# The expert stage of a graph and mixture-of-experts kernel: one TensorE signal a step, seven steps deep instead of five

## The chip, the cores and the metric

The kernel runs on one core of a Trainium2 chip. The metric is the time of one execution on the device in microseconds (us). Before the change it is 2094.08, the median of three runs (2093.04 to 2095.15).

## What is computed

The input is x (128 graphs of 128 nodes, 384 values a node, fp32) and an adjacency matrix a graph. A two-layer graph network comes first and is not touched. Then follows the expert layer, which the change is about:

```python
xt = layernorm(x).reshape(-1, 384)                  # 16384 tokens
route_prob = softmax((xt @ enc_w + enc_b) @ sw_w + sw_b)
routes = argmax(route_prob)                         # one of 8 experts
h = gelu(xt @ w1[expert] + b1[expert])              # 384 -> 64
out = (h @ w2[expert] + b2[expert]) * max(route_prob)   # 64 -> 384
x = x + out
```

## The kernel before

Two blocks follow each other. The first computes the graph network over the 128 graphs, decides each token's expert, and scatters each token's row (its 384 values, then the layer norm's scale and shift, the probability and the token's number: 388 words) into DRAM buckets, one for each expert. The second block, the expert stage (from line 1357), works through 72 tiles of 256 tokens, each of one expert. A tile has T = 2 halves of 128 tokens, and a feature row has C = 3 chunks of 128.

Each engine has its own instruction stream, which a Python loop writes out in full: `tiles` calls `step(i)` for i from 0 to 76, and in step i an engine works on the tile that the pipeline's depth gives it. The order within an engine is the order of the calls; between engines there are only semaphores. For tile j:

- SyncE (`load`, L1421) loads the tile's rows into `tok[j % 8]`. From tile 8 on it waits until the results (`y_ready`) and ids of tile j - 8 are done.
- ScalarE and VectorE (`normalise`, L1492 and L1541, step j) scale and shift one half each into `n2_rows`.
- TensorE (`turn`, step j + 1) transposes the six 128 x 128 pieces, the first two chunks into one PSUM bank and the third into another (L1445), and signals `turned`.
- ScalarE copies expert and bias weights (`pick_w1`, L1500 and L1504) and the first two chunks (`copy_first`, L1510), VectorE the third (`copy_last`, L1548), into `n2T`, still in step j + 1.
- TensorE (`hidden`, step j + 2, L1457) multiplies by w1: three products of 256 columns, then signals `hidden_done`.
- ScalarE takes the gelu (`gelu`, L1519, step j + 2). VectorE splits it into a high and a low part (`gelu_high`, L1554, and `gelu_low`, L1558, step j + 2).
- GpSimd adds up the row numbers for the store (`keep_ids`, L1597, step j + 2).
- TensorE (`output`, step j + 4, L1469 and L1470) makes two products of 384 columns for each half, and signals `y_done` for each half. Each half has one PSUM bank and waits until VectorE has read that half of the tile before (`y_ready`).
- VectorE (`combine`, L1567, step j + 5) scales the result, adds the token's row, writes `out_rows[j % 4]` and signals `y_ready` for each half.
- GpSimd (`store`, L1607, step j + 5) writes each half to its tokens' places with an indirect DMA, for which it makes the descriptors itself.

Within a step TensorE does turn, hidden, output. ScalarE does normalise, pick, copy, gelu; VectorE does combine, normalise, copy, split. So ScalarE copies what TensorE turned in the same step, and takes the gelu of what TensorE multiplied in the same step. SyncE waits at the end for all stores (L1431), and a barrier ends the program (L1412).

## Time and profile before

| | |
|---|---|
| median of three runs | 2094.08 us |
| the profiled execution's own time | 2095.15 us |
| its span, first to last instruction | 2093.4 us |
| mean granted TensorE clock | 0.989 |
| busy: TensorE, VectorE, ScalarE, GpSimd | 97%, 81%, 70%, 67% |
| expert stage: first transposes, last results, last store | 1885.70, 2082.25, 2089.22 us |
| token loads, indirect stores | 72 of 388 KB, 144 |

The profile is one execution, with times counted from its first instruction. The durations below come from it alone; its own time is 1.07 us above the median of the runs. In its rows PE is TensorE, DVE VectorE, ACT ScalarE, POOL GpSimd and SP SyncE, and buffer numbers are left out of names: `bank` is any PSUM bank, `n_rows` is n2_rows, `w_top` is w2_top, `w_pick` is w1_pick. A matmul of full fp32 is recorded as two, so that `x6` at L1457 is three products. The end of a matmul is modelled, so the distance between starts is what tells its cost.

### The profile page before, as it was taken

How to read it: one execution, taken by the hardware profiler on the slowest of the kernel's cores; microseconds unless marked ns; L12 is line 12 of the kernel's file. 1: busy time of each engine (PE TensorE's matmuls, PEld its weight loads, DVE VectorE, ACT ScalarE, POOL GpSimd, SP SyncE). 2: the span in 40 equal slices, each digit the busy share in tenths (PEclk: the TensorE clock that was granted, in tenths of full speed). 3: DMA queues.
4: the chain of work that ended last, by engine and by line, in shares of the span. 5: the costliest groups of instructions: out<-in, count | busy, mean ns of one | idle time of the engine just before them, and what ended most of it. 6: DMA issues, size and time to landing. Idle time of an engine off the chain costs nothing. (4 is left out here: it accounts for less than half of the span.)

```text
span 2093.4 us, 48362 instructions
## 1 busy us (share of the span) xinstructions
PE 2029.2 (97%) x12059; PEld 1880.2 (90%) x12059; DVE 1689.7 (81%) x5206; ACT 1468.5 (70%) x3804; POOL 1403.7 (67%) x3342
## 2 busy tenths in 40 slices
PE   5999999999999999999999999999999999959997
PEld 4988899999999999999999999999999999948996
DVE  4788888888888888888888888888888888758997
ACT  4777777777677777777777776777777777627775
POOL 2556666666766666666666676666676666646887
PEclk9999999999999999999999999999999999979999
DMA  7011111221111111111111111111111111118895
GB/s 200 24 37 43 48 43 44 87 81 43 52 52 44 51 52 52 43 48 48 46 45 52 48 43 52 51 43 52 52 49 42 52 48 39 39 64 260 281 297 187
DMA packets 94358, 153.43 MB, mean 73 GB/s; under 512 B 17621, under 2 KB 70875, under 8 KB 94082
## 3 DMA queue, kind: packets, MB, share of 16 engines
q1 hardware_dynamic: 75972, 99.61, 16.4%
q0 software_dynamic: 17408, 50.62, 6.3%
q8 instruction: 103, 1.69, 0.3%
q14 instruction: 171, 1.40, 0.2%
q10 hardware_dynamic: 704, 0.10, 0.0%
HBM read 96.11 MB, written 57.32 MB: 73 GB/s over the span
## 5 line engine op out<-in xcount | busy, mean ns | idle before, releaser
L422 PE MATMUL bank<-wT_hi,own_hi 128*128 128x384 f32 x1536 | 513.6, 334 | 2.4 <-ACT bank L646 2.4
L424 PE MATMUL bank<-wT_hi,own_lo 128*128 128x384 f32 x1536 | 514.1, 335 | 0.0
L423 PE MATMUL bank<-wT_lo,own_hi 128*128 128x384 f32 x1536 | 513.2, 334 | 0.0
L436 PE MATMUL bank<-own_hi 128*128 128x512 f32 x768 | 324.0, 422 | 6.3 <-ACT bank L660 6.1
L438 PE MATMUL bank<-own_hi,own_lo 128*128 128x512 f32 x768 | 302.7, 394 | 0.0
L437 PE MATMUL bank<-own_lo,own_hi 128*128 128x512 f32 x768 | 300.2, 391 | 0.0
L422 PEld LDWEIGHTS bank<-wT_hi,own_hi 128*128 128x128 f32 x1536 | 288.4, 188 | 3.1 <-issue 1.9
L423 PEld LDWEIGHTS bank<-wT_lo,own_hi 128*128 128x128 f32 x1536 | 288.4, 188 | 0.0
L424 PEld LDWEIGHTS bank<-wT_hi,own_lo 128*128 128x128 f32 x1536 | 288.3, 188 | 0.0
L667 ACT ACTIVATE bank<-bank,sum_own 128x384 f32<-128x384 f32 x256 | 141.2, 552 | 206.7 <-issue 177.1
L1190 POOL TENSOR_TENSOR own_lo<-hT,own_hi 128x384 fp32r<-128x384 f32 x256 | 260.6, 1018 | 19.0 <-ACT own_hi L710 18.6
L1272 POOL TENSOR_TENSOR var_e<-mv,denom_sq 128x1 f32<-128x1 f32 x256 | 48.6, 190 | 235.7 <-DVE mv L858 235.6
L639 ACT ACTIVATE bank<-bank,neg_max 128x128 f32<-128x128 f32 x256 | 87.6, 342 | 164.6 <-DVE neg_max L826 164.6
L841 DVE CUSTOM_DVE_ANT_0 diagonal<-delta,ident 128x128 f32<-128x128 f32 x256 | 177.6, 694 | 9.0
L438 PEld LDWEIGHTS bank<-own_hi,own_lo 128*128 128x128 f32 x768 | 144.4, 188 | 33.3
L436 PEld LDWEIGHTS bank<-own_hi 128*128 128x128 f32 x768 | 145.1, 189 | 30.2 <-issue 7.2
L1607 POOL DMA_INDIRECT out_dram<-out_rows,row_ids x144 | 142.5, 989 | 43.9 <-issue 26.4
L1247 POOL TENSOR_SCALAR_AFFINE_SELECT deltaT_hi<-turned_hi 128x128 fp32r<-128x128 f32 x256 | 75.1, 293 | 141.7 <-ACT turned_hi L691 138.8
L660 ACT COPY bank<-own_seed 128x512 f32<-128x512 f32 x256 | 151.3, 591 | 22.5 <-ACT bank L667 0.4
L437 PEld LDWEIGHTS bank<-own_lo,own_hi 128*128 128x128 f32 x768 | 145.8, 190 | 22.9
L1236 POOL DMA_INDIRECT buckets<-rows,dest_words x128 | 138.8, 1084 | 29.4 <-issue 25.0
L863 DVE SCALAR_TENSOR_TENSOR bank<-bank,mv,gamma 128x384 f32<-128x384 f32 x256 | 157.9, 617 | 0.0
(213 smaller groups left out, 5590.1 us busy)
## 6 DMA issues: line engine op xcount, KB each, us to landing
tok<-buckets SPq DMA_DIRECT2D x72, 388.0 KB
x_in<-in_x_dram SPq DMA_DIRECT2D x128, 192.0 KB, 2.6
x_res<-in_x_dram SPq DMA_DIRECT2D x128, 192.0 KB
adj_in<-in_adj_dram SPq DMA_DIRECT2D x128, 64.0 KB, 2.6
buckets<-pads SPq DMA_DIRECT2D x9, 388.0 KB
out_dram<-out_rows,row_ids POOLq DMA_INDIRECT x144
buckets<-rows,dest_words POOLq DMA_INDIRECT x128, 2.8
w_top<-in_L_ffn_w_dram SPq DMA_DIRECT2D x2, 768.0 KB
```

Source lines behind the costliest of these rows:

```text
L422: pe.matmul(o, hi, w_hi(l, m, c), start=False, stop=False, skip_group_check=True)
L423: pe.matmul(o, hi, w_lo(l, m, c), start=False, stop=False, skip_group_check=True)
L424: last = pe.matmul(o, lo, w_hi(l, m, c), start=False, stop=(c == C - 1), skip_group_check=True)
L436: pe.matmul(own_bank[:], hi, own_w_hi, start=False, stop=False, skip_group_check=True)
L437: pe.matmul(own_bank[:], hi, own_w_lo, start=False, stop=False, skip_group_check=True)
L438: last = pe.matmul(own_bank[:], lo, own_w_hi, start=False, stop=(c == C - 1), skip_group_check=True)
L660: act.copy(own_bank[:], own_seed[:, u[1], WINDOW[k]]).then_inc(selfseed_ready, 1)
L667: act.activation(ctx_banks[odd][:, 0:D], own_bank[:, SELF[odd]], ACT.Copy, scale=sum_own[odd][:, 0:1]).then_inc(selfterm_ready, 1)
L841: dve.tensor_tensor_reduce(diagonal[:], delta[:], ident[:], 1.0, 0.0, ALU.mult, ALU.add, sum_own[odd][:]).then_inc(own_ready, 1)
L863: dve.scalar_tensor_tensor(o, o, mv[odd][:, 0:1], gamma[:, w[1], :], ALU.subtract, ALU.mult).then_inc(centred, 1)
L1190: pool.tensor_tensor(own_lo[:, l, :, SLOT[odd]], hT[:].rearrange("p (c t) -> p c t", c=C), own_hi[:, l, :, SLOT[odd]].bitcast(F32), ALU.su ...
L1607: pool.indirect_dma_start(out.rearrange("b s d -> (b s) d"), bass.IndirectOffsetOnAxis(ap=row_ids[k][:, t:t + 1].bitcast(U32), axis=0), ou ...
```

## The change

The pipeline grows from five steps to seven, and TensorE increments one semaphore, `products_done`, on the last matmul of its step, in place of `turned`, `hidden_done` and twice `y_done`. Whoever needs a product of TensorE waits until the step that made it has ended and so works in the next step: turning in step j + 1 as before, copies in j + 2, hidden products in j + 3, gelu in j + 4, split and row ids in j + 5, output products in j + 6, results and stores in j + 7. TensorE does hidden, turn, output within a step. ScalarE begins a step with the copy, then gelu, normalise, pick; VectorE does copy, combine, normalise, split.

The eight PSUM banks are dealt anew: two for the first two chunks, one (was two) for the third, two for hidden products, three (was two) for the results, taken in turn over the halves. `n2_rows`, `w1_pick` and `b1_pick` have three buffers instead of two, `tok` and `row_ids` twelve instead of eight, so SyncE may load twelve tiles before it waits. The core of the diff (the like edits of `normalise`, `pick_w1`, `gelu`, the splits, `keep_ids` and `store` are left out; the last two are called in steps j + SPLIT and j + DEPTH):

```diff
-    OUT_RING = 4
-    tok = ring_sb(RING, "tok", [P, T, WORDS])
-    n2_rows = ring_sb(2, "n2_rows", [P, T, D])
+    OUT_RING, HELD = 4, 12
+    assert TILES % HELD == 0
+    tok = ring_sb(HELD, "tok", [P, T, WORDS])
+    n2_rows = ring_sb(3, "n2_rows", [P, T, D])
...
-    w1_pick = ring_sb(2, "w1_pick", [P, C, 2, R])
-    b1_pick = ring_sb(2, "b1_pick", [P, 1])
+    w1_pick = ring_sb(3, "w1_pick", [P, C, 2, R])
+    b1_pick = ring_sb(3, "b1_pick", [P, 1])
...
-    y_done, y_ready = sem("y_done"), sem("y_ready")
-
-    turn_banks = ((bank[0], bank[1]), (bank[2], bank[3]))
-    hidden_banks = (bank[4], bank[5])
-    y_banks = (bank[6], bank[7])
-
-    OUTPUT, GELUS, DEPTH = 4, 4, 5
...
+    products_done, y_ready = sem("products_done"), sem("y_ready")
+
+    first_banks, last_bank = (bank[0], bank[1]), bank[2]
+    hidden_banks = (bank[3][:, 0:TILE], bank[4][:, 0:TILE])
+    y_banks = (bank[5], bank[6], bank[7])
+
+    PICK, TURN, COPY, HIDDEN, GELU, SPLIT, OUTPUT, DEPTH = 1, 1, 2, 3, 4, 5, 6, 7
+    GELUS = 4
...
+            def load(j):
+                k = j % HELD
                 row = sp.value_load(tile_row[0:1, j:j + 1], min_val=0, max_val=TAIL)
-                if past(j, RING):
-                    sp.wait_ge(y_ready, T * (j - RING) + T)
+                if j >= HELD:
+                    sp.wait_ge(y_ready, T * (j - HELD) + T)
                     sp.nop(nofuse=True)
-                    sp.wait_ge(ids_kept, j - RING + 1)
...
-            def turn(j, k):
+            def turn(j):
                 pe.wait_ge(n2_act_ready, j + 1)
                 pe.wait_ge(n2_dve_ready, j + 1)
-                if past(j, 2):
+                if j >= 2:
                     pe.wait_ge(first_copied, j - 1)
-                    pe.wait_ge(last_copied, j - 1)
-                first, last_bank = turn_banks[k % 2]
                 for c in range(C):
-                    o = first[:, c * TILE:(c + 1) * TILE] if c < 2 else last_bank[:, 0:TILE]
+                    if c == 2 and j >= 1:
+                        pe.wait_ge(last_copied, j)
+                    o = first_banks[j % 2][:, c * TILE:(c + 1) * TILE] if c < 2 else last_bank[:, 0:TILE]
                     for t in range(T):
                         last = pe.transpose(o[:, t * P:(t + 1) * P],
-                                            n2_rows[k % 2][:, t, c * P:(c + 1) * P], ident[:])
-                last.then_inc(turned, 1)
-
-            def hidden(j, k):
+                                            n2_rows[j % 3][:, t, c * P:(c + 1) * P], ident[:])
+                return last
+
+            def hidden(j):
                 pe.wait_ge(w1_picked, j + 1)
                 pe.wait_ge(first_copied, j + 1)
                 pe.wait_ge(last_copied, j + 1)
-                if past(j, 2):
+                if j >= 2:
                     pe.wait_ge(gelu_ready, j - 1)
-                o = hidden_banks[k % 2][:, 0:TILE]
                 for c in range(C):
-                    last = pe.matmul(o, w1_pick[k % 2][:, c, :, :].rearrange("p h r -> p (h r)"),
-                                     n2T[k % 2][:, c, :], start=(c == 0), stop=(c == C - 1))
-                last.then_inc(hidden_done, 1)
-
-            def output(j, k):
+                    last = pe.matmul(hidden_banks[j % 2], w1_pick[j % 3][:, c, :, :].rearrange("p h r -> p (h r)"),
+                                     n2T[j % 2][:, c, :], start=(c == 0), stop=(c == C - 1))
+                return last
+
+            def output(j):
                 e = expert_in(words, j)
                 pe.wait_ge(gelu_top_ready, j + 1)
                 pe.wait_ge(gelu_bottom_ready, j + 1)
                 for t in range(T):
-                    if past(j, 1):
-                        pe.wait_ge(y_ready, T * (j - 1) + t + 1)
-                    o, rows = y_banks[t][:, 0:D], slice(t * P, (t + 1) * P)
-                    pe.matmul(o, gelu_top[k % GELUS][:, rows], w2_top[:, e, :], start=True, stop=False)
-                    pe.matmul(o, gelu_bottom[k % GELUS][:, rows], w2_bottom[:, e, :], start=False, stop=True
-                              ).then_inc(y_done, 1)
-
-            def step(i, k):
-                if there(i - 1):
-                    turn(i - 1, k - 1)
-                if there(i - 2):
-                    hidden(i - 2, k - 2)
+                    n = T * j + t
+                    if n >= 3:
+                        pe.wait_ge(y_ready, n - 2)
+                    o, rows = y_banks[n % 3][:, 0:D], slice(t * P, (t + 1) * P)
+                    pe.matmul(o, gelu_top[j % GELUS][:, rows], w2_top[:, e, :], start=True, stop=False)
+                    last = pe.matmul(o, gelu_bottom[j % GELUS][:, rows], w2_bottom[:, e, :], start=False, stop=True)
+                return last
+
+            def step(i):
+                if there(i - HIDDEN):
+                    last = hidden(i - HIDDEN)
+                if there(i - TURN):
+                    last = turn(i - TURN)
                 if there(i - OUTPUT):
-                    output(i - OUTPUT, (k - OUTPUT) % RING)
+                    last = output(i - OUTPUT)
+                if TURN <= i < TILES + OUTPUT:
+                    last.then_inc(products_done, 1)

             pe.wait_ge(tiles_ready, 2)
             words = read_words(pe)
@@ -1485,48 +1486,50 @@
...
+            def copy_first(j):
+                act.wait_ge(products_done, j + TURN)
+                if j >= 2:
...
-            def step(i, k):
+                act.activation(gelu_out[j % 2][:], hidden_banks[j % 2], ACT.Gelu,
+                               bias=b1_pick[j % 3][:, 0:1]).then_inc(gelu_ready, 1)
+
+            def step(i):
+                if there(i - COPY):
+                    copy_first(i - COPY)
+                if there(i - GELU):
+                    gelu(i - GELU)
                 if there(i):
-                    normalise(i, k)
-                if there(i - 1):
-                    pick_w1(i - 1, k - 1)
-                    copy_first(i - 1, k - 1)
-                if there(i - 2):
-                    gelu(i - 2, k - 2)
+                    normalise(i)
+                if there(i - PICK):
+                    pick_w1(i - PICK)

             act.wait_ge(tiles_ready, 2)
             words = read_words(act)
@@ -1534,50 +1537,52 @@
...
+            def copy_last(j):
+                dve.wait_ge(products_done, j + TURN)
+                if j >= 2:
+                    dve.wait_ge(products_done, j - 2 + HIDDEN)
...
-            def combine(j, k):
+            def combine(j):
+                k, n = j % HELD, j % OUT_RING
+                dve.wait_ge(products_done, j + OUTPUT)
                 for t in range(T):
...
-            def step(i, k):
+            def step(i):
+                if there(i - COPY):
+                    copy_last(i - COPY)
                 if there(i - DEPTH):
-                    combine(i - DEPTH, (k - DEPTH) % RING)
+                    combine(i - DEPTH)
                 if there(i):
-                    normalise(i, k)
-                if there(i - 1):
-                    copy_last(i - 1, k - 1)
-                if there(i - 2):
-                    gelu_high(i - 2, k - 2)
-                    gelu_low(i - 2, k - 2)
+                    normalise(i)
+                if there(i - SPLIT):
+                    gelu_high(i - SPLIT)
+                    gelu_low(i - SPLIT)

             for k in range(GELUS):
                 dve.memset(gelu_bottom[k][HIGH:P, :].bitcast(F32), 0.0).then_inc(ones_set, 1)
@@ -1589,17 +1594,17 @@
```

On TensorE one step of the steady part stood so before (L1445 turns, L1457 is hidden, L1469 and L1470 are the output, whose `REGISTER_ALU` and `ISA` rows work out the expert's place in w2):

```order
L1445 MATMUL bank<-ident,n_rows 128x128 [waits first_copied,last_copied,n2_dve_ready,n2_act_ready]
L1445 MATMUL bank<-ident,n_rows 128x128 x5
L1457 MATMUL bank<-n2T,w_pick 128x256 [waits last_copied,gelu_ready,first_copied,w1_picked]
L1457 MATMUL bank<-n2T,w_pick 128x256 x2
L1469 REGISTER_ALU [waits y_ready,gelu_bottom_ready,gelu_top_ready]
L1469 REGISTER_ALU
L1469 ISA
L1469 MATMUL bank<-w_top,gelu_top 128x384
L1470 REGISTER_ALU
L1470 MATMUL bank<-w_bottom,gelu_bottom 128x384
L1469 MATMUL bank<-w_top,gelu_top 128x384 [waits y_ready]
L1470 MATMUL bank<-w_bottom,gelu_bottom 128x384
```

and stands so now (L1455 hidden, L1444 turns, L1468 and L1469 output):

```order
L1455 MATMUL bank<-n2T,w_pick 128x256 [waits last_copied,gelu_ready,first_copied,w1_picked]
L1455 MATMUL bank<-n2T,w_pick 128x256 x2
L1444 MATMUL bank<-ident,n_rows 128x128 [waits first_copied,n2_dve_ready,n2_act_ready]
L1444 MATMUL bank<-ident,n_rows 128x128 x3
L1444 MATMUL bank<-ident,n_rows 128x128 [waits last_copied]
L1444 MATMUL bank<-ident,n_rows 128x128
L1468 REGISTER_ALU [waits y_ready,gelu_bottom_ready,gelu_top_ready]
L1468 REGISTER_ALU
L1468 ISA
L1468 MATMUL bank<-w_top,gelu_top 128x384
```

The hidden products moved ahead of the transposes, and the wait for VectorE's copy of the third chunk moved from the first transpose to the fifth.

On ScalarE, at the start of the stage, before (L1510 copies the first two chunks, L1492 normalises, L1500 and L1504 pick weights, L1519 is the gelu):

```order
L1510 COPY n2T0<-bank0 128x512 [waits turned]
L1492 ACTIVATE n2_rows2<-tok2 128x384 [waits turned,tok_loaded2]
L1500 REGISTER_ALU x2
L1500 ISA
L1500 COPY w1_pick1<-w1_all 128x384
L1504 ISA
L1504 COPY b1_pick1<-b1_col 128x1
L1510 COPY n2T1<-bank2 128x512 [waits turned]
L1519 ACT_TABLE_LOAD [waits b1_picked]
L1519 ACTIVATE gelu_out0<-bank4,b1_pick0 128x256 [waits hidden_done]
```

and now, from the second copy on:

```order
L1512 COPY n2T1<-bank1 128x512 [waits products_done]
L1494 ACTIVATE n2_rows0<-tok3 128x384 [waits products_done,tok_loaded3]
L1502 REGISTER_ALU x2
L1502 ISA
L1502 COPY w1_pick2<-w1_all 128x384
L1506 ISA
L1506 COPY b1_pick2<-b1_col 128x1
L1512 COPY n2T0<-bank0 128x512 [waits products_done]
L1521 ACT_TABLE_LOAD [waits b1_picked]
L1521 ACTIVATE gelu_out0<-bank3,b1_pick0 128x256 [waits products_done]
```

The load of the gelu's table and the first gelu moved from behind the second copy to behind the third, and that copy waits for TensorE's third step.

## Rows read from the trace of the kernel before

**Rows 1.** The page, busy time of each engine, with its share of the span

```profile
PE 2029.2 (97%) x12059; PEld 1880.2 (90%) x12059; DVE 1689.7 (81%) x5206; ACT 1468.5 (70%) x3804; POOL 1403.7 (67%) x3342
```

**Rows 2.** Busy time by stretch: stretch, engines, granted clock, DMA share, GB/s

```profile
1905.00:2055.00 150.00, 150.00 (x904) 138.76 (x903) 140.39 (x340) 115.46 (x282) 122.01 (x169) 1.00 0.92 291
```

**Rows 3.** Timeline of TensorE, one step: start, us, engine, line, operation

```profile
1951.16 0.82 PE L1445 MATMUL bank<-ident,n_rows 128*128 128x128 f32 x6
1951.81 1.46 PE L1457 MATMUL bank<-n2T,w_pick 128*128 128x256 f32 x6
...
1953.28 0.34 PE L1470 MATMUL bank<-w_bottom,gelu_bottom 128*128 x1
1953.46 0.34 PE L1469 MATMUL bank<-w_top,gelu_top 128*128 x1
1953.63 0.34 PE L1470 MATMUL bank<-w_bottom,gelu_bottom 128*128 x1
1953.81 0.82 PE L1445 MATMUL bank<-ident,n_rows 128*128 128x128 f32 x6
```

**Rows 4.** Timeline of GpSimd in the steady part: three stores, and one after a stall

```profile
1953.97 1.01 POOL L1607 DMA_INDIRECT out_dram<-out_rows,row_ids  x1 [0.16 <-POOL row_ids L1597]
1955.28 0.97 POOL L1607 DMA_INDIRECT out_dram<-out_rows,row_ids  x1 [0.30 <-issue]
...
1956.63 1.00 POOL L1607 DMA_INDIRECT out_dram<-out_rows,row_ids  x1 [0.16 <-POOL row_ids L1597]
...
2049.54 0.97 POOL L1607 DMA_INDIRECT out_dram<-out_rows,row_ids  x1 [1.51 <-DVE out_rows L1567]
```

**Rows 5.** Timeline of GpSimd at the start: the first store of tiles 0, 1 and 2

```profile
1897.28 1.01 POOL L1607 DMA_INDIRECT out_dram<-out_rows,row_ids  x1 [9.02 <-DVE out_rows L1567]
...
1900.23 0.99 POOL L1607 DMA_INDIRECT out_dram<-out_rows,row_ids  x1 [0.20 <-issue]
...
1902.93 0.99 POOL L1607 DMA_INDIRECT out_dram<-out_rows,row_ids  x1 [0.16 <-issue]
```

**Rows 6.** Timeline of the end: GpSimd's stores, VectorE's last results

```profile
2077.60 0.99 POOL L1607 DMA_INDIRECT out_dram<-out_rows,row_ids  x1 [0.16 <-issue]
...
2080.26 0.99 POOL L1607 DMA_INDIRECT out_dram<-out_rows,row_ids  x1 [0.16 <-issue]
...
2082.25 1.14 DVE L1567 SCALAR_TENSOR_TENSOR out_rows<-bank,tok 128x384 f32<-128x384 f32 x2 [0.66 <-PE bank L1470]
...
2087.94 0.97 POOL L1607 DMA_INDIRECT out_dram<-out_rows,row_ids  x1 [0.30 <-issue]
2089.22 0.97 POOL L1607 DMA_INDIRECT out_dram<-out_rows,row_ids  x1 [0.31 <-issue]
```

**Rows 7.** Timeline of TensorE at the start: the second tile's hidden products

```profile
1891.10 1.46 PE L1457 MATMUL bank<-n2T,w_pick 128*128 128x256 f32 x6
```

**Rows 8.** Timeline of ScalarE at the start: the second copy, table load, first gelu

```profile
1888.83 0.58 ACT L1510 COPY n2T<-bank 128x512 f32<-128x512 f32 x1
1889.43 1.28 ACT L1519 ACT_TABLE_LOAD   x1
1890.72 0.47 ACT L1519 ACTIVATE gelu_out<-bank,b_pick 128x256 f32<-128x256 f32 x1
```

**Rows 9.** Timeline of VectorE: results of tiles 0, 1, 2, a result and copy, tile 67

```profile
1895.83 1.12 DVE L1567 SCALAR_TENSOR_TENSOR out_rows<-bank,tok 128x384 f32<-128x384 f32 x2
...
1898.79 1.13 DVE L1567 SCALAR_TENSOR_TENSOR out_rows<-bank,tok 128x384 f32<-128x384 f32 x2
...
1901.21 1.12 DVE L1567 SCALAR_TENSOR_TENSOR out_rows<-bank,tok 128x384 f32<-128x384 f32 x2
...
1949.69 0.60 DVE L1567 SCALAR_TENSOR_TENSOR out_rows<-bank,tok 128x384 f32<-128x384 f32 x1
...
1950.60 0.41 DVE L1548 COPY n2T<-bank 128x256 f32<-128x256 f32 x1
...
2074.09 1.13 DVE L1567 SCALAR_TENSOR_TENSOR out_rows<-bank,tok 128x384 f32<-128x384 f32 x2
```

More of the change, by code:

```diff
@@ L1372, in build @@
             out_rows = ring_sb(OUT_RING, "out_rows", [P, T, D])
-            row_ids = ring_sb(RING, "row_ids", [P, T], I32)
-            tok_loaded = [sem(f"tok_loaded{k}") for k in range(RING)]
+            row_ids = ring_sb(HELD, "row_ids", [P, T], I32)
+            tok_loaded = [sem(f"tok_loaded{k}") for k in range(HELD)]
             stored = [sem(f"stored{k}") for k in range(OUT_RING)]
@@ L1405, in there @@
             def there(j):
-                return not isinstance(j, int) or 0 <= j < TILES
-            def past(j, n):
-                return not isinstance(j, int) or j >= n
+                return 0 <= j < TILES
             with nc.Block() as block:
@@ L1487, in _, with normalise @@
                 def _(act):
-                    def normalise(j, k):
-                        act.wait_ge(tok_loaded[k], 16 // RING * (j - k) + 16)
-                        if past(j, 2):
-                            act.wait_ge(turned, j - 1)
-                        act.activation(n2_rows[k % 2][:, 0, :], tok[k][:, 0, 0:D], ACT.Identity,
+                    def normalise(j):
+                        k = j % HELD
+                        act.wait_ge(tok_loaded[k], 16 * (j // HELD) + 16)
+                        if j >= 3:
+                            act.wait_ge(products_done, j - 3 + TURN)
+                        act.activation(n2_rows[j % 3][:, 0, :], tok[k][:, 0, 0:D], ACT.Identity,
@@ L1493, in normalise, with pick_w1 @@
                                        bias=tok[k][:, 0, SHIFT:SHIFT + 1], scale=tok[k][:, 0, SCALE:SCALE + 1]
                                        ).then_inc(n2_act_ready, 1)
-                    def pick_w1(j, k):
+                    def pick_w1(j):
                         e = expert_in(words, j)
-                        if past(j, 2):
-                            act.wait_ge(hidden_done, j - 1)
-                        act.copy(w1_pick[k % 2][:], w1_all[:, e, :, :].unsqueeze(2).broadcast_to([P, C, 2, R])
+                        if j >= 3:
+                            act.wait_ge(products_done, j - 3 + HIDDEN)
+                        act.copy(w1_pick[j % 3][:], w1_all[:, e, :, :].unsqueeze(2).broadcast_to([P, C, 2, R])
@@ L1501, in pick_w1 @@
                                  ).then_inc(w1_picked, 1)
-                        if past(j, 2):
-                            act.wait_ge(gelu_ready, j - 1)
-                        act.copy(b1_pick[k % 2][:], b1_col[:, bass.ds(e, 1)]).then_inc(b1_picked, 1)
-                    def copy_first(j, k):
-                        act.wait_ge(turned, j + 1)
-                        if past(j, 2):
-                            act.wait_ge(hidden_done, j - 1)
-                        act.copy(n2T[k % 2][:, 0:2, :].rearrange("p c t -> p (c t)"), turn_banks[k % 2][0][:, 0:2 * TILE]
+                        if j >= 3:
+                            act.wait_ge(gelu_ready, j - 2)
@@ L1511, in copy_first, with gelu @@
+                        act.copy(b1_pick[j % 3][:], b1_col[:, bass.ds(e, 1)]).then_inc(b1_picked, 1)
+                    def copy_first(j):
+                        act.wait_ge(products_done, j + TURN)
+                        if j >= 2:
+                            act.wait_ge(products_done, j - 2 + HIDDEN)
+                        act.copy(n2T[j % 2][:, 0:2, :].rearrange("p c t -> p (c t)"), first_banks[j % 2][:, 0:2 * TILE]
                                  ).then_inc(first_copied, 1)
-                    def gelu(j, k):
-                        act.wait_ge(hidden_done, j + 1)
+                    def gelu(j):
+                        act.wait_ge(products_done, j + HIDDEN)
@@ L1536, in _ @@
                 def _(dve):
-                    def normalise(j, k):
-                        dve.wait_ge(tok_loaded[k], 16 // RING * (j - k) + 16)
-                        if past(j, 2):
-                            dve.wait_ge(turned, j - 1)
-                        dve.tensor_scalar(n2_rows[k % 2][:, 1, :], tok[k][:, 1, 0:D], tok[k][:, 1, SCALE:SCALE + 1],
-                                          tok[k][:, 1, SHIFT:SHIFT + 1], ALU.mult, ALU.add).then_inc(n2_dve_ready, 1)
-                    def copy_last(j, k):
-                        dve.wait_ge(turned, j + 1)
-                        if past(j, 2):
-                            dve.wait_ge(hidden_done, j - 1)
-                        dve.tensor_copy(n2T[k % 2][:, 2, :], turn_banks[k % 2][1][:, 0:TILE]).then_inc(last_copied, 1)
```

74 lines of the change are left out of this document (39 added, 35 removed).

## The prediction

> **What bounds the kernel now.** I read first the row of busy times of the whole kernel [rows 1]: TensorE is at work 97% of the span, so only its own work or what it waits for can matter. The expert stage, which alone is changed, is the last tenth of the span. A table of one long stretch of it [rows 2] has TensorE busy for 150.00 of 150.00 us at the full granted clock, VectorE for 140.39, GpSimd for 122.01, and the DMA engines at a share of 0.92. There is no idle TensorE time in that stretch to win back.
>
> Next the timeline of one step on TensorE [rows 3]. From the first transpose at 1951.16 to the next step's at 1953.81 is 2.65 us: 0.65 for six transposes (to 1951.81), and then 2.00 until 1953.81, in which three hidden products of 256 columns and four output products stand. The last four starts are 0.18, 0.17 and 0.18 apart, so I count 4 x 0.176 = 0.70 for the outputs and 1.30 for the hidden products. Sum 0.65 + 1.30 + 0.70 = 2.65: the step is its matmuls and nothing else, and 72 steps are 191 us.
>
> TensorE is not what ends the program, though. VectorE's last pair of results runs from 2082.25 for 1.14, to 2083.39; the last store goes out at 2089.22 [rows 6]. GpSimd writes descriptors for two indirect stores per token tile and is behind by 5.8 us. In the middle its tiles are 1956.63 - 1953.97 = 2.66 us apart [rows 4]. Near the end the results lie ready 2.9 us ahead (the first of a tile at 2074.09 + 0.60 = 2074.69 [rows 9], its store at 2077.60), and a tile with its row ids still takes 2080.26 - 2077.60 = 2.66; one without ids, beside an idle VectorE, takes 2 x 1.28 = 2.56 (2089.22 - 2087.94 = 1.28) [rows 6]. So **GpSimd has the same pace as TensorE and never makes up a delay**: the end is the start of the first store (1897.28 [rows 5]), plus 71 tiles at GpSimd's pace, plus its stalls, plus 4.2 us from the last store's start to the end of the span. One stall stands in the last of [rows 4]: the store at 2049.54 has 1.51 idle before it where others have 0.30.
>
> **The change, part by part.**
> *Signals.* Each TensorE step gave four (turned, hidden_done, two of y_done) and now gives one. In [rows 3] the matmul at 1953.46 has no signal and its follower starts 0.17 later; those at 1953.28 and 1953.63 have one and are followed after 0.18 and 0.18; six transposes of which the last signals take 6 x 0.109. The price of a signal is between 0 and 0.01 us, at most 3 x 0.01 x 72 = 2.2 us on TensorE. I take 0, since the spacings are equal within the rows' rounding. Whatever it gives on TensorE, the end follows only down to GpSimd's own tile: beside an idle VectorE a store takes 1.28 and not 1.31 (1955.28 - 1953.97 [rows 4]), which makes the tile 2.66 - 2 x 0.03 = 2.60, so that at most 71 x 0.06 = 4.3 us could come out at the end.
> The Trainium skill, page "TensorE: Matmul & The Clock Gate", section "The cost: per-tile semaphore tail", says that increments on packed matmuls serialise at 26.3 ns each and advises a single one on the last; by that figure, as an estimate, three fewer would be worth 3 x 26.3 ns x 72 = 5.7 us of TensorE time, 4.3 at the end, and the sum below would be -1.4 in place of +2.9. The rows' 0.18 against 0.17 don't bear that out for matmuls this long.
>
> *One step later.* Every consumer now waits for the end of the step before. In the steady state this costs nothing as long as each has a slack: hidden products want a copy that starts right after the signal of the step before last (a whole step to spare). The tightest is the new single bank for the third chunk: TensorE's fifth transpose in a step waits for VectorE's copy of the tile before, which starts on the signal of the step just ended. The signal is some 0.16 after the last matmul's stream, the copy takes 0.41 [rows 9], and TensorE meanwhile has 1.30 of hidden products and 0.44 of transposes: slack 1.74 - 0.57 = 1.2 us. The second output product of a step wants VectorE's first result of the same step: 0.16 + 0.41 + 0.60 = 1.2 after the step's start, needed at 1.30 + 0.65 + 0.35 = 2.3, slack 1.1. VectorE itself has 2.49 of work in a step of 2.66 (140.39 / 150 [rows 2]), so it is free when the signal comes. Cost 0; if that cover went, each 0.01 us a step would be 0.7 us.
>
> *Order hidden, turn, output.* The same thirteen matmuls in another order: 0.
>
> *Buffers.* Twelve token buffers let SP issue twelve loads at once and then run five steps ahead (three before). The bytes are the same; loads 8 to 11 are issued behind those that the first tiles need. Cost 0, and if the DMA engines (0.92 busy) delay something, GpSimd's stores have four out_rows buffers, about 10 us. A third n2_rows, w1_pick and b1_pick: 0.
>
> *The longer fill is the one price that I find.* The first store waits for the first result, and that moves from TensorE's step 4 to step 6, with VectorE in step 7. Up to 1891.10, where the turning of tile 2 ends, nothing changes: same order, same waits [rows 7]. Then
> - step 4, hidden products and turning: 1.30 + 0.65, to 1893.05;
> - step 5 wants the first gelu. ScalarE's table load, which stood right behind the second copy, now stands behind the third copy, which waits for the signal of step 3 at about 1891.26. Copy to load 0.60, load 1.28, gelu 0.47 [rows 8]: 1893.61, so TensorE waits 0.6 there, to 1893.7;
> - step 5, 1.95: 1895.65; step 6, 2.65: 1898.3, with a last bubble of 0.1 for a gelu that is just behind: 1898.4;
> - signal 0.16, copy 0.41, first result 0.60: 1899.5. The store began 0.85 after the first result's end before (1895.83 + 0.60 = 1896.43 [rows 9] to 1897.28), and again does: 1900.4.
>
> So the first store is **3.1 us later**. Bounds: 2.5 if the table load is hidden after all, 3.7 if ScalarE is that much later again. Two corrections. The second tile's store came 1900.23 - 1897.28 = 2.95 after the first [rows 5], because the result did; now it can follow after 2.66: -0.3. The last tiles without row ids are two instead of three: +0.1. **Sum +2.9 us.** TensorE and VectorE will end somewhat earlier than before, since the tail of outputs alone is longer, but GpSimd does not follow.
>
> The profiled execution took 2095.15 (its span 2093.4 and 1.75 around it), 1.07 above the median of 2094.08. On the median: 2094.08 + 2.9 = **2097.0 us**, +0.14%. I take 0.2%, 4.2 us, as the least that a measurement of this kernel tells from no change.
>
> **The rivals.**
> *A. GpSimd's pace gets worse (slower).* VectorE's order becomes copy, two results, normalise, two splits, and GpSimd meets other neighbours. The trace has GpSimd tiles of 2.70 that no late result explains: 1902.93 - 1900.23 [rows 5], while the results were 1901.21 - 1898.79 = 2.42 apart [rows 9]. If all 71 went so: 71 x 0.045 = +3.2, in all +6.1, 2100.2 us. It decides from 0.018 us a tile. Against it: the pace was 2.66 in the middle and again near the end, after the stall had moved the stores against VectorE's operations.
> The Trainium skill, page "SBUF — State Buffer", section "SBUF: two separate sides", has VectorE and GpSimd share a port pair under an exclusive lock. The 1.28 beside an idle VectorE against 1.30 beside a busy one would agree; by that rule it matters which VectorE operation a store meets, and the change reorders them.
> *B. TensorE's step gets shorter (no change).* If the signals cost 0.01 each, GpSimd's 2.60 would let it through: +2.9 - 2.2 = +0.7, 2094.8 us. For it only the rounding of the rows.
> *C. TensorE waits in every step (slower)*, for the copy of the third chunk or for a result, because VectorE falls behind. With VectorE at 2.70 a step: 72 x 0.045 = +3.2, in all 2100.2. Against it the slacks of 1.1 and more; it needs VectorE's 2.49 to grow past 2.66.
> *D. Faster.* The ends of matmuls are modelled, so a bubble could be hidden in the 2.65, and GpSimd may be held by VectorE for all that its 2.66 is above 2.56. Then 71 x 0.10 = -7.1, in all -4.2, 2089.9 us. Against it the row ids, whose time stays.
>
> **How the numbers follow.** Forecast 0.57, of which 0.08 lies above +4.2 (a store that locks into a later phase or a longer fill). A 0.19, nearly all above +4.2. B 0.12. C 0.07, of which 0.05 above. D 0.05. Slower by over 0.2%: 0.08 + 0.17 + 0.05 = 0.30; faster 0.05; within 0.2% the other 0.65. The range: below, the shortest fill and B, 2.5 - 0.2 - 2.2 = +0.1, 2094.2; above, A with a little of a longer fill, 2100.6. The forecast's own range is +2.3 to +4.3, 2096.4 to 2098.4.
>
> **What would show it.** Right: TensorE's steps at 2.65 to 2.66 in the new profile with no idle time between; the first store near 1900.4 and the table load after the third copy; stores 2.66 a tile; last result before 2083.4, last store near 2092, a lag of 9 us. Wrong: idle time of TensorE ended by the copy at L1552 or by out_rows; steps under 2.64; a store pace of 2.68 or more; a first store before 1899 or after 1901.5; or stores that catch up with the results.

## The result, and the profile after

Over 20 runs of each kernel the changed one takes 2097.8 us (median; 2095.85 to 2099.69) and the kernel before 2094.9 (2093.04 to 2096.42). The ratio is 1.0014, 95% interval 1.0008 to 1.0020: **+2.9 us**, slower, but by less than 0.2%. On the median of 2094.08 shown before, the ratio gives 2097.0. The profiled execution took 2096.4 with a span of 2094.7; before it was 2095.15 and 2093.4.

The whole kernel and the same long stretch, answering to [rows 1, 2] (page, part 1, and the table of one stretch: us, busy of each engine with its count, granted clock, DMA share, GB/s), of the changed kernel:

```profile
PE 2027.1 (97%) x12059; PEld 1877.9 (90%) x12059; DVE 1691.8 (81%) x5206; ACT 1467.9 (70%) x3804; POOL 1404.2 (67%) x3342
```

```profile
1905.00:2055.00 150.00, 150.00 (x907) 138.38 (x906) 143.95 (x340) 116.04 (x284) 122.69 (x169) 1.00 0.91 290
```

TensorE is again busy throughout at the full granted clock. One step of it, answering to [rows 3]; timeline of TensorE (start us, duration us, engine line op, tiles, count, idle before with what ended it):

```profile
1952.39 1.46 PE L1455 MATMUL bank<-n2T,w_pick 128*128 128x256 f32 x6
1953.68 0.82 PE L1444 MATMUL bank<-ident,n_rows 128*128 128x128 f32 x6
1954.26 0.42 PE L1468 MATMUL bank<-w_top,gelu_top 128*128 x1
1954.52 0.34 PE L1469 MATMUL bank<-w_bottom,gelu_bottom 128*128 x1
1954.69 0.34 PE L1468 MATMUL bank<-w_top,gelu_top 128*128 x1
1954.87 0.34 PE L1469 MATMUL bank<-w_bottom,gelu_bottom 128*128 x1
1955.04 0.38 PE L1455 MATMUL bank<-n2T,w_pick 128*128 128x256 f32 x1
```

A step is 1955.04 - 1952.39 = 2.65, no idle time in it. No time is lost in such a step; most of the loss lies before the first store. The fill on TensorE and ScalarE, answering to [rows 7, 8]:

```profile
1889.22 1.46 PE L1455 MATMUL bank<-n2T,w_pick 128*128 128x256 f32 x6
1890.52 0.82 PE L1444 MATMUL bank<-ident,n_rows 128*128 128x128 f32 x6
1891.99 1.53 PE L1455 MATMUL bank<-n2T,w_pick 128*128 128x256 f32 x6 [0.66 <-ACT gelu_out L1521]
1893.36 0.82 PE L1444 MATMUL bank<-ident,n_rows 128*128 128x128 f32 x6
```

```profile
1889.47 0.58 ACT L1512 COPY n2T<-bank 128x512 f32<-128x512 f32 x1 [0.85 <-PE bank L1444]
1890.08 1.28 ACT L1521 ACT_TABLE_LOAD   x1
1891.37 0.47 ACT L1521 ACTIVATE gelu_out<-bank,b_pick 128x256 f32<-128x256 f32 x1
```

The table load stands behind the third copy, which waited 0.85 for the end of TensorE's step, and TensorE then waits for the first gelu. The first result and stores, answering to [rows 5, 9] (VectorE and GpSimd):

```profile
1897.28 1.13 DVE L1572 SCALAR_TENSOR_TENSOR out_rows<-bank,tok 128x384 f32<-128x384 f32 x2
```

```profile
1898.74 1.15 POOL L1612 DMA_INDIRECT out_dram<-out_rows,row_ids  x1 [13.02 <-DVE out_rows L1572]
1900.19 0.98 POOL L1612 DMA_INDIRECT out_dram<-out_rows,row_ids  x1 [0.30 <-issue]
1901.17 0.33 POOL L1603 TENSOR_TENSOR row_ids<-tok,again 128x2 int32<-128x2 int32 x1
1901.66 1.00 POOL L1612 DMA_INDIRECT out_dram<-out_rows,row_ids  x1 [0.15 <-issue]
```

The expert stage began 1.9 us earlier in this execution than in the one before (in the profiled executions of this study its first hidden matmul lies between 1885.7 and 1889.8), so absolute positions can't be compared. I count from that matmul, 1888.28 before and 1886.39 here. The first store is at 9.00 before and at 12.35 now, **3.35 later**.

GpSimd's one long stall, answering to the last of [rows 4]. I call it the halt:

```profile
2047.27 0.97 POOL L1612 DMA_INDIRECT out_dram<-out_rows,row_ids  x1 [0.30 <-DVE out_rows L1572]
2048.26 0.21 POOL L1603 TENSOR_TENSOR row_ids<-tok,again 128x2 int32<-128x2 int32 x1
2048.62 0.99 POOL L1612 DMA_INDIRECT out_dram<-out_rows,row_ids  x1 [0.16 <-issue]
2050.54 1.01 POOL L1612 DMA_INDIRECT out_dram<-out_rows,row_ids  x1 [0.92 <-DMA out_dram<-out_rows,row_ids]
```

And the end, answering to [rows 6]:

```profile
2083.50 1.14 DVE L1572 SCALAR_TENSOR_TENSOR out_rows<-bank,tok 128x384 f32<-128x384 f32 x2 [2.29 <-DMA out_dram<-out_rows,row_ids]
...
2089.19 0.97 POOL L1612 DMA_INDIRECT out_dram<-out_rows,row_ids  x1 [0.30 <-issue]
2090.47 0.97 POOL L1612 DMA_INDIRECT out_dram<-out_rows,row_ids  x1 [0.30 <-issue]
```

The last result waits 2.29 for an out_rows buffer whose stores have landed: Here VectorE, and with it TensorE, is held back by GpSimd through the four buffers.

The positions of all kernels, in us from the stage's first hidden matmul, worked out from their traces. "Result 57" is the start of tile 57's first result (counting from 0), "lag" the time from the end of a tile's first result to its first store, at tile 56 (before the halt) and at 57 (after it); "step" is TensorE's mean step between tiles 2 and 57 as the results show it. The last column is against the kernel before, run beside it; 0.0010 is 2.1 us.

```
kernel             first store  step    result 57  lag 56  lag 57  last store  ratio of times (95%)
before                  9.00    2.660    159.25     1.55    2.76     200.93
changed                12.35    2.653    162.13     2.15    2.80     204.08    1.0014 (1.0008 to 1.0020)
late_store             11.66    2.713    162.36     3.86    3.98     205.73    1.0017 (1.0008 to 1.0026)
late_ring6             11.66    2.656    159.26     3.77    3.77     202.36    1.0006 (0.9997 to 1.0016)
more_signals           12.34    2.653    162.12     2.34    2.80     204.06    1.0015 (1.0006 to 1.0024)
early_table            11.49    2.653    161.27     2.15    2.80     203.22    1.0011 (1.0001 to 1.0020)
depth_six              10.53    2.653    160.31     1.28    2.80     203.43    1.0009 (0.9999 to 1.0018)
six_early               9.37    2.653    159.15     1.27    2.80     201.40    1.0002 (0.9993 to 1.0011)
ids_act_before          9.44    2.706    161.90     0.83    2.93     203.75    1.0012 (1.0003 to 1.0021)
ids_act_after          12.74    2.653    162.42     0.91    2.73     204.01    1.0010 (1.0001 to 1.0019)
few_rows8              12.49    2.653    162.12     2.38    2.38     205.20    (one run)
few_rows16             12.62    2.653    162.26     2.37    2.38     205.00    (one run)
few_rows16_before       9.15    2.659    159.08     1.62    1.62     202.14    (one run)
```

Times of runs scatter by some 2 us, while positions in a trace can repeat to a few hundredths (changed and more_signals), so sizes below are taken from positions and the times only have to agree. One thing limits this: in the six- and seven-step kernels with full stores the mark lies between 2.68 (six_early) and 3.11 (ids_act_after) ahead of tile 1's first hidden matmul, and 2.83 in the changed kernel, so a difference of some 0.3 between two rows can be the mark's own. The expectations count from other marks: those of late_store and early_table from tile 1's first hidden matmul (2.82 after mine), those of later runs from the fourth of tile 0's six hidden matmuls (1.28 after mine, 0.76 in late_ring6).

### The profile page after: what moved, and what is told of

Its sections match the earlier page's. It is cut to its first block and busy times, and to the rows that moved or that the text cites. A ratio compares the mean times of both kernels' runs of the same rounds, so it can differ in the third digit from the quotient of the medians.

```text
span 2094.7 us, 48286 instructions
## 1 busy us (share of the span) xinstructions
PE 2027.1 (97%) x12059; PEld 1877.9 (90%) x12059; DVE 1691.8 (81%) x5206; ACT 1467.9 (70%) x3804; POOL 1404.2 (67%) x3342
## 3 DMA queue, kind: packets, MB, share of 16 engines
q8 instruction: 103, 1.69, 0.3%
```

## The experiments

**The fill and the end.** The kernel before, its first store made late by a wait:

```diff
 pool.wait_ge(ids_kept, j + 1)
+if j == 0:
+    pool.wait_ge(y_ready, T + 1)
```

> The kernel before with one wait added: GpSimd's first store also waits for the first result of tile 1, so that it is issued about one step later; no other engine waits for anything new. Theory (GpSimd sets the end with its own pace of 2.66 us a tile and never makes up a delay): first store 2.7 us later after the stage's first products of tile 1 (8.9 us in place of 6.2), last store 2.7 us later, kernel 2.4 to 2.9 us slower than before, about all of the difference that the change made. Rival (TensorE and VectorE end the program, GpSimd only follows): the stores close up during the stage, the last store moves by under 1 us and the kernel is 0 to 1 us slower.

The first store came 2.66 later, as meant, but the last one 4.80. Both theories had less. Waits of VectorE in the middle stretch (us in all, times, longest):

```profile
DVE out_rows L1567 <- DMA out_dram<-out_rows,row_ids: 3.8, 11, 0.6
```

With stores a step later, the four out_rows buffers no longer sufficed; the changed kernel has no such wait in that stretch. So the run also bore a second price. The same with six buffers (`OUT_RING = 6`, indices and counts by tile):

> The kernel before with the late first store again and six out_rows buffers in place of four. Theory (the late store cost 4.8 us at the end in place of 2.7 because VectorE, with stores one step later, waited for out_rows buffers whose stores hadn't landed, 3.8 us in the middle stretch): no wait of VectorE for a landing, TensorE's steps back at 2.66 from 2.72, first store 10.4 us after the stage's first product, last store at 202.3 to 202.8 in place of 204.45. Rival (stores that lag 3.5 us or more meet VectorE's operations at a worse place and take longer): store steps stay at 2.71 or more and the last store near 204.5.

The waits for landings are gone and steps are 2.656. The first store is late by 2.66, the last one by only 1.43: below the 2.7 that I expected, and the rival (store steps of 2.71) fell too. The reason stands in the columns of lags. GpSimd ran 3.77 behind from tile 4 on, and where the others halt at tile 56 it did not. Its 114th store, the second of tile 56, in late_ring6:

```profile
2050.60 0.99 POOL L1609 DMA_INDIRECT out_dram<-out_rows,row_ids  x1 [0.16 <-issue]
2051.90 0.97 POOL L1609 DMA_INDIRECT out_dram<-out_rows,row_ids  x1 [0.30 <-issue]
```

The halt costs the kernel before 1.21, the changed one 0.65, six_early 1.53, ids_act_after 1.82, and the two kernels that are over 2.8 behind none (late_ring6 0.00) or next to none (late_store 0.12). In seven of the eight kernels that halt at this store it ends 2.01 or 2.02 after tile 57's first result began (2.24 in ids_act_before); in late_ring6 that store comes only 3.01 after it. The delay of late_ring6 against the kernel before was 2.22 at tile 56, 1.01 at tile 57, and grew again to 1.43 by the last store. **A delay of GpSimd alone is partly made up at the halt; a delay of the results is not.** From result 57 to the last store it is 41.68 before and 41.95 in the changed kernel.

**The signals.** The changed kernel with three more increments a step, on matmuls that had none, of a semaphore without a reader:

```diff
 last = hidden(i - HIDDEN)
+if there(i - OUTPUT):
+    last.then_inc(unused, 1)
 last = turn(i - TURN)
+if there(i - OUTPUT):
+    last.then_inc(unused, 1)
...
 last = pe.matmul(o, gelu_bottom[...], w2_bottom[...], start=False, stop=True)
+if t == 0:
+    last.then_inc(unused, 1)
```

> The changed kernel with three more increments a step on TensorE, on a semaphore that nobody waits for, behind the hidden product, the turn and the first token half's product. Theory (signals on full-size products cost nothing beside them): steps of TensorE stay at 2.65 us, the kernel within 0.5 us of the changed one. My own bound of 0.01 us for each would give +2.2 us on TensorE, and at the kernel's end less, since GpSimd paces it. Rival (each signal holds TensorE some 26 ns, the Trainium skill's figure in TensorE: Matmul & The Clock Gate, The cost: per-tile semaphore tail): steps of 2.73 us, the kernel 5 us slower than the changed one, as TensorE becomes the slower engine.

The long stretch on TensorE:

```profile
1950.17 1.46 PE L1456 MATMUL bank<-n2T,w_pick 128*128 128x256 f32 x6
1951.46 0.82 PE L1445 MATMUL bank<-ident,n_rows 128*128 128x128 f32 x6
1952.03 0.42 PE L1469 MATMUL bank<-w_top,gelu_top 128*128 x1
...
1952.82 1.02 PE L1456 MATMUL bank<-n2T,w_pick 128*128 128x256 f32 x4
```

1952.82 - 1950.17 = 2.65, the mean 2.653 as in the changed kernel, the last store 0.02 earlier. Signals without a waiter on matmuls of 128 to 384 columns cost nothing that shows, so the changed kernel's 0.007 shorter step hardly comes from fewer of them; its new order, its later waits or its banks are left, and which wasn't tried.

**The table load.** One small activation ahead of the stage:

```diff
+act.activation(gelu_out[0][:, 0:1], ident[:, 0:1], ACT.Gelu)
 act.wait_ge(tiles_ready, 2)
 words = read_words(act)
```

> The changed kernel with one small Gelu activation on ScalarE before it waits for the expert stage (its result is overwritten), so that the table load of 1.28 us falls before the stage. Theory (the table load behind the third copy makes TensorE wait 0.66 us in the first steps, and GpSimd never makes it up): the wait of the fourth hidden product for gelu_out goes, the first store comes 0.6 us earlier after the first products of tile 1 (8.9 in place of 9.5 us), and the kernel is 0.5 to 0.7 us faster than the changed one. Rival (the fill isn't on the path that sets the end): first store 0.6 earlier, end unmoved.

```profile
1889.20 1.46 PE L1455 MATMUL bank<-n2T,w_pick 128*128 128x256 f32 x6
1890.50 0.82 PE L1444 MATMUL bank<-ident,n_rows 128*128 128x128 f32 x6
1891.15 1.46 PE L1455 MATMUL bank<-n2T,w_pick 128*128 128x256 f32 x6
```

TensorE's wait is gone (1891.15 follows 1890.50 by 0.65). First store, result 57 and last store all come 0.86 earlier: the gain passes through in full, as the theory says, and is a little above my 0.6.

**The seventh step.** Split, output, results and stores one step earlier, all else as changed:

```diff
-PICK, TURN, COPY, HIDDEN, GELU, SPLIT, OUTPUT, DEPTH = 1, 1, 2, 3, 4, 5, 6, 7
+PICK, TURN, COPY, HIDDEN, GELU, SPLIT, OUTPUT, DEPTH = 1, 1, 2, 3, 4, 4, 5, 6
```

> The changed kernel with GeLU's split, the output products, the results and the stores one step earlier (six steps from a tile's turn to its store, not seven; the output products then wait for a split made in the same step); signals, banks and buffers stay as changed. Theory (the seventh step costs one step of fill, signals and buffers nothing, and the slack of about 1.1 us in a step suffices for TensorE's products to wait for a split of the same step): first store and last store 2.65 us earlier than in the changed kernel, kernel 2.4 to 2.9 us faster than it, within 0.5 us of before. Rival (the seventh step is needed: TensorE then waits for the split in each step, 0.1 to 0.5 us): steps of TensorE over 2.66 us with waits for gelu_bottom, the kernel 5 us or more slower than before.

The steps stay at 2.653 without waits: the seventh isn't needed for the steady state. But it is worth 1.82 at the first store (1.94 counted from tile 1's first hidden matmul, where the mark plays no part) and not 2.65. I had counted a full step; a step of the fill has no output products (1.30 for hidden, see 1889.22 to 1890.52 above, and 0.65 for turns). At the last store only 0.65 of it was left. The rest went in two GpSimd tiles before the end, whose stores took longer (timeline of GpSimd):

```profile
2061.58 1.40 POOL L1612 DMA_INDIRECT out_dram<-out_rows,row_ids  x1 [0.16 <-issue]
2063.29 0.97 POOL L1612 DMA_INDIRECT out_dram<-out_rows,row_ids  x1 [0.30 <-issue]
2064.27 0.51 POOL L1603 TENSOR_TENSOR row_ids<-tok,again 128x2 int32<-128x2 int32 x1
2064.94 1.12 POOL L1612 DMA_INDIRECT out_dram<-out_rows,row_ids  x1 [0.16 <-issue]
```

Both edits together:

> The six-step version of the changed kernel with the early table load as well. Theory (both save in the fill and don't overlap: 1.82 for the seventh step, 0.86 for the table load as each measured alone): first store 8.4 us after the stage's first product (changed kernel 11.07, before 7.72); last store between 200.0 (GpSimd in its 2.66 throughout) and 201.3 (it loses the 1.2 us again that the six-step run lost in steps of 2.8 and 3.4 us near its end). Kernel 1.4 to 2.7 us faster than the changed one, 0.3 to 1.5 slower than before. Rival (the fill's gains aren't seen at the end since GpSimd loses them again): last store above 201.5.

First store at 9.37 (from my later mark 8.09, expected 8.4), last store 2.68 earlier than in the changed kernel and 0.47 later than before; in time 1.0002 (0.9993 to 1.0011), no difference from the kernel before that these runs can tell. Counted from tile 1's first hidden matmul the first store lies at 9.52 in the changed kernel, 8.64 in early_table, 7.58 in depth_six, 6.69 here and 6.18 before: the two parts add up (0.88 + 1.94 against 2.83) and carry most of the 3.34. The remaining 0.5, for which the wait for a whole step's end and VectorE's copy ahead of its results are the likely grounds, no run took apart. The version doesn't beat the kernel before.

**GpSimd relieved.** Row ids made on ScalarE, two activations a tile (Identity, with `again` as a float bias), nothing but stores on GpSimd; the like edit in both kernels, in step j + 3 of the five-step kernel and step j + 5 of the seven-step one (shown for the latter, `again` made as floats):

```diff
-pool.tensor_tensor(row_ids[k][:], tok[k][:, :, ID].bitcast(I32), again[:, j, :], ALU.add
-                   ).then_inc(ids_kept, 1)
+for t in range(T):
+    act.activation(row_ids[k][:, t:t + 1], tok[k][:, t, ID:ID + 1].bitcast(I32), ACT.Identity,
+                   bias=again[:, j, t:t + 1]).then_inc(ids_kept, 1)
```

> The kernel before with the row ids of a tile made on ScalarE (two small activations, which has some 0.6 us to spare in each step) and not on GpSimd, so that GpSimd only issues the stores. Theory (GpSimd's own pace of 2.66 us a tile sets the end, of which the ids are 0.06): GpSimd's own tile becomes 2.60, below TensorE's 2.65, so that stores close up with the results after each stall (lag of the 67th tile's store 0.9 to 1.1 us in place of 2.9), TensorE's steps stay at 2.66, and only the last five tiles' stores run at GpSimd's pace: last store 2.0 us earlier, kernel 1.5 to 2.2 us faster than before. Rival (GpSimd isn't held by its own instructions but by VectorE or the DMA engines beside it): stores stay 2.66 apart and as far behind, the kernel within 0.5 us of before; if ScalarE becomes late, TensorE's steps grow over 2.67.

> The changed kernel with the same edit: row ids on ScalarE, GpSimd only stores. Theory: first store as in the changed kernel (11.1 us after the stage's first product), stores close up, last store 2.0 to 2.2 us earlier than there; kernel 1.5 to 2.3 us faster than the changed one and still 2.5 to 3.3 us slower than the kernel before with the same edit, since the longer fill stays on the path of both. Rival (the price of the change was GpSimd's own, so a GpSimd with slack makes it up): the two kernels with the edit end within 1 us of each other.

Stores did close up before the halt (lag 0.83 and 0.91; a tile of 2.58 where one is behind), and neither kernel gained; the five-step one became slower, with its last store 2.82 later than before. Of the changed kernel the halt took back nearly all: lag 2.73 after it, last store 0.07 earlier (0.35 counted from tile 1's first hidden matmul). Behind the halt neither closed up again: tiles took 2.66 in the one, and six of ten 2.72 in the other, and lags stayed at 2.7 to 3.0 up to tile 66. In the kernel before ScalarE came late, and TensorE with it. Its waits (us in all, times, longest), its long stretch, and then that of the changed kernel with the edit:

```profile
PEld bank L1469 <- issue: 5.4, 19, 0.4
DVE gelu_top L1566 <- ACT gelu_out L1529: 4.6, 18, 0.4
```

```profile
1905.00:2055.00 150.00, 149.96 (x887) 134.85 (x886) 141.04 (x334) 133.64 (x388) 110.39 (x110) 1.00 0.92 285
```

```profile
1905.00:2055.00 150.00, 150.00 (x906) 138.21 (x905) 140.59 (x339) 137.31 (x395) 113.77 (x113) 1.00 0.91 291
```

TensorE got through 887 matmuls in the five-step kernel and 906 in the seven-step one: steps of 2.706 against 2.653, with ScalarE busy for 133.64 and 137.31. **This is what the change buys**: a step that bears 0.4 us more on ScalarE. Which part of it does that (the later waits, the order, the buffers) these two runs don't separate, and the ids also stand two steps later in the one. The two kernels with the edit end 0.26 apart at the last store, as the rival had said, though not by its mechanism: GpSimd made nothing up, TensorE's slower steps in the one ate the shorter fill.

**The halt.** Stores of 2 rows in place of 128 in the first 8 or 16 tiles, so that most of these tiles' rows are missing from the output; one execution of each:

```diff
+m = 2 if j < 8 else P          # or j < 16
...
-row_ids[k][:, t:t + 1] ... out_rows[n][:, t, :]
+row_ids[k][0:m, t:t + 1] ... out_rows[n][0:m, t, :]
```

> The changed kernel, but the stores of the first 8 token tiles write 2 rows each in place of 128 (the other rows of these tiles are left out of the output); all else as changed. It asks where GpSimd's halt of tile 56 comes from, which in every run so far stands before the 114th store, even with a third of GpSimd's instructions taken away. If it comes from a count of descriptors (16 x 126 = 2016 fewer, the work of 16 stores), it moves to about the 130th store, tile 64. If it comes from the number of store instructions or from something that the other engines do at that time, it stays at tile 56, and its end stays 2.0 us after the start of tile 57's first result. Last store within 0.5 us of the changed kernel's (202.8 after the stage's first product) either way.

> The same with the first 16 tiles (32 stores with 2 rows, 4032 descriptors fewer, the work of 32 stores; the other rows of these tiles are left out). If the halt goes by descriptors, it would come at the 146th store, which there is not: the lag of tile 57 stays at 2.1 us or below in place of 2.80, and the last store comes 0.6 to 1.5 us earlier than in the changed kernel. If it goes by tile or by instructions, it stays.

> The kernel before with the same edit: 2 rows in place of 128 in each store of the first 16 tiles, the other rows left out. If the halt goes by descriptors: none at tile 56, lag of tile 57 1.5 us in place of 2.76, last store 1.2 us earlier after the stage's first product (198.4 in place of 199.65), and the difference to the changed kernel with the same edit 2.5 to 4 us at the last store. If it goes by tile or by instructions, it stays.

The halt left tile 56 and stood ahead of tile 63's first store (the 127th) with 8 short tiles, and of tile 64's (the 129th) with 16, in both kernels. GpSimd in the changed kernel with 16:

```profile
2068.59 0.97 POOL L1613 DMA_INDIRECT out_dram<-out_rows,row_ids  x1 [0.30 <-issue]
2069.58 0.21 POOL L1603 TENSOR_TENSOR row_ids<-tok,again 128x2 int32<-128x2 int32 x1
2071.31 0.99 POOL L1613 DMA_INDIRECT out_dram<-out_rows,row_ids  x1 [1.52 <-DVE out_rows L1572]
```

So it isn't tied to a count of store instructions, nor to what the other engines do at tile 56. It moves with what the stores before it wrote, but not one for one (13 and 15 stores for the work of 16 and 32), so that what is counted stays open. Moved, it brought the lag to 3.8 and not 2.8, in both kernels, and the last stores came about 1 us later, not earlier as I expected. Part of that can be read off: the halt again ends at nearly the same place against the results, 1.69 to 1.74 after the next tile's first result began (2.01 at tile 56), but the store it holds is now the first of its tile and not the second, so one store more, 1.30, still stands ahead of the next tile. What fixes that place is open. The price of the change stayed about the same: 205.00 - 202.14 = 2.86 with the halt moved, 3.15 with it in place.

## Why the prediction was right, point by point

*Result.* Forecast 2097.0 (+2.9), measured +2.9. At the last store the traces say 204.08 - 200.93 = +3.15. That the number fits so well is in part luck, as the points below show: the mechanism of the fill was right, two terms behind it were wrong and offset each other.

*Signals: 0.* Right, by more_signals: three more increments a step moved nothing. The Trainium skill, "TensorE: Matmul & The Clock Gate", "The cost: per-tile semaphore tail", gives 26.3 ns each on packed matmuls; for the larger matmuls of this kernel, which it doesn't speak of, the traces show no such price.

*One step later, order, buffers: 0 in the steady state.* Right: no idle TensorE time in the long stretch, no engine late. TensorE's step even came out 0.007 shorter, 0.38 by tile 57, which I hadn't in the sum.

*The fill: +3.1.* Right in mechanism and place, 3.35 in size. Counted from tile 1's first hidden matmul, tile 2's starts at 2.77 (1891.99 - 1889.22) where the sum had 2.6, so the wait behind the table load was 0.82 and not 0.65; the small second bubble of 0.1 is in the next step, 2.02 long. The first result came 0.61 after its step's end, 0.57 expected.

*The corrections: -0.3 and +0.1.* The first did not come: tile 1's store still stands 2.92 behind the first (1901.66 - 1898.74), because the first store took 1.15 and the row ids 0.33. In its place the results caught up from 3.34 late at tile 0 to 2.88 at tile 57, of which 0.38 by TensorE's shorter steps. The second came: tile 69, now with row ids, took 2.66 in place of 2.57. With that tile, one of 2.79 at tile 66 and a lag greater by 0.04 behind the halt, result 57 to last store is 0.27 longer, and 2.88 + 0.27 = 3.15. That the results' gain was nearly as large as the correction that failed was luck.

*"GpSimd never makes up a delay", and the end as first store plus 71 tiles plus stalls.* **This step was wrong**, though the sum was right. I took the halt for a constant. It is 1.21 long before and 0.65 after, and leaves both kernels 2.8 behind the results; late_ring6 kept only 1.43 of the 2.66 that it was made late. The price reached the end because the results were late by 2.88 at tile 57, from which the end of the halt keeps its distance of 2.01, not because the stores were. TensorE's gain in pace reached it in the same way.

*"TensorE and VectorE will end somewhat earlier", "last result before 2083.4", "a lag of 9 us".* Wrong. The last results began at 2083.50, held for 2.29 by the out_rows buffers, and 3.1 later from the stage's mark than before (197.11 against 193.97); the last store followed their end by 2090.47 - 2084.64 = 5.8. I had named the four buffers and not applied them to the tail. My marks in absolute time were also badly chosen: the first store came at 1898.74, by the letter before the 1899 that was to show me wrong, but the stage began 1.89 earlier in this execution, and 1898.74 + 1.89 = 1900.6 against the 1900.4 forecast.

*Rivals.* A: up to the halt four late store tiles of 2.71 to 3.08 (20, 33, 34, 51), else 2.66 behind tile 1; they brought the lag to 2.15, and the halt would have taken it to 2.80 anyway. GpSimd's work took 1.15 for the first store and 0.33 for the row ids behind it, against 0.97 to 1.00 and 0.21 in most tiles, where VectorE was no less busy (143.95 of 150 in the long stretch). The Trainium skill ("SBUF — State Buffer", "SBUF: two separate sides") has some VectorE operations lock GpSimd out of a shared port pair and others not; that would allow such differences, but no run here isolates it. B: the step did get shorter, by 0.007, and it was seen at the end, but not by the signals, for which more_signals shows no price. C: no waits. D: fell; GpSimd without ids did follow VectorE closely and gained nothing.

## What to carry to other kernels

A deeper pipeline is paid once, in the fill: look for what each extra fill step holds (here some 1.9, not the full 2.65), and for one-time work such as a table load that the new order pushes onto the path (0.86 here, which one early activation removes). Ask what it could win: here TensorE had no idle time, and a gain showed only once ScalarE was given more to do. Before you say that a late follower sets the end, look for points where versions fall in at the same distance behind: for those that come to it closer than that, it is the engine followed that counts up to there.

## What the runs showed of the hardware

- An increment that nobody waits for, on a matmul of 128 to 384 columns, costs under 0.001 us: steps of 2.653 with one increment and with four, and result 57 within 0.01 (changed, more_signals).
- A GpSimd store of 128 rows mostly takes 0.97 to 1.00, and a tile's second follows its first after 1.28 to 1.30; two stores and the ids of a tile take 2.66; without the ids 2.56 to 2.58. With 2 rows in place of 128 the second still follows after 1.16 to 1.23, so most of the time doesn't depend on the number of rows.
- GpSimd halts once in the stage, at the 114th store in the eight kernels with full stores that come to it 0.8 to 2.3 behind the results, and goes on 2.7 to 2.9 behind them (2.0 to 2.2 after tile 57's first result began); the two kernels that were 3.8 and 3.9 behind pass without a halt. Taking its row-id work away did not move it; writing fewer rows earlier did. What it waits for, no run shows.
